# A graph layer over 50,000 nodes: the second weight applied before the edge sum, in a first pass over DRAM

## The reference

```python
_layernorm(x) = (x - mean) / sqrt(var + 1e-05)          # over the 256 features
# graph layer, on xn = _layernorm(x); edge_index = stack([src, dst])
agg  = segment_sum(xn[dst], src)                        # for each node, over its edges
mean = agg / maximum(segment_sum(1, src), 1)[:, None]
x = x + xn @ W1.T + b1 + mean @ W2.T + b2
# feed-forward, on h = _layernorm(x)
all_out = experts_mlp(h, ...)      # 4 experts, 256 -> 128 -> 64 -> 256, relu
shared  = shared_mlp(h, ...)       # 256 -> 256 -> 128 -> 256, relu
gates = softmax(h @ gW + gb); the two largest, softmax over them
x = x + shared + sum of the two chosen experts' outputs by those weights
```

## Time and profile before

| what | value |
|---|---|
| time, median of 3 runs | 4213.46 us (4186.71 to 4247.7) |
| span of the profiled execution | 4086.2 us |
| the profiled execution's own launch time | not given; the three runs lie 100.5 to 161.5 us above its span |
| instructions | 72214 |
| TensorE busy | 3755.7 us, 92% |
| VectorE busy | 3509.2 us, 86% |
| GpSimd busy | 2756.4 us, 67% |
| ScalarE busy | 2236.2 us, 55% |
| granted TensorE clock, mean | 0.955 |
| DMA, mean | 39 GB/s |

### The profile page before, as it was taken

The page is one execution under the profiler, slowest core; times in us unless marked ns, Lnnn a source line. Parts: engine busy times, 40 slices in busy tenths (PEclk is TensorE's granted clock), DMA queues, the critical chain, the costliest instruction groups (busy, mean ns, idle before and its releaser), DMA issues.

```text
span 4086.2 us, 72214 instructions
## 1 busy us (share of the span) xinstructions
PE 3755.7 (92%) x20644; PEld 2987.0 (73%) x20644; DVE 3509.2 (86%) x8557; ACT 2236.2 (55%) x4286; POOL 2756.4 (67%) x2275
## 2 busy tenths in 40 slices
PE   4677599999999999999999999999999999999998
PEld 2222387877788787777877788788878878778776
DVE  8999788888888888888888888888888888888886
ACT  1455355555565555555655555555655555555554
POOL 3044576777777777776777777777777777777762
PEclk6699899999999999999999999999999999999999
DMA  1000111111111111111111111111111111111110
GB/s 33 0 0 0 40 47 45 42 35 45 46 45 45 42 42 38 45 45 40 45 35 45 45 45 45 38 41 41 46 45 45 45 36 41 44 45 45 42 34 19
DMA packets 52637, 157.42 MB, mean 39 GB/s; under 512 B 13637, under 2 KB 14327, under 8 KB 52602
## 3 DMA queue, kind: packets, MB, share of 16 engines
q1 hardware_dynamic: 28602, 105.73, 7.7%
q0 software_dynamic: 24000, 51.29, 4.4%
HBM read 120.06 MB, written 51.20 MB: 42 GB/s over the span
## 4 chain that ended last, share of the span: by engine, by line
PE 44%; DVE 18%; issue 12%; POOL 8%; ACT 4%; another core or an unknown queue 2%; DVEq 1%; POOLq 0%; ACTq 0%
PE bank L1032 12%; PE bank L1008 10%; PE bank L985 9%; DVE h_lo L1256 5%; PE bank L866 5%; PE bank L925 4%; POOL l_var L774 3%; POOL l_rstd L784 3%; DVE x1n_sb L1314 3%; PE bank L959 2%; DVE x_sb L1191 2%; ACT h_hi L1096 1%; ACT xT_hi L915 1%; DVE l_mv L1303 1%
## 5 line engine op out<-in xcount | busy, mean ns | idle before, releaser
L826 POOL TENSOR_SCALAR e_oh<-iota_sb,cols 128x500 fp32r<-128x500 f32 x490 | 836.1, 1724 | 20.8 <-POOL cols L820 20.8
L985 PE MATMUL bank<-x1T_hi,wl_hl 128*128 128x500 f32 x2400 | 669.7, 394 | 0.0
L796 POOL DMA_INDIRECT rows<-in_x,slots x500 | 517.3, 1035 | 211.2 <-issue 98.8
L774 POOL TENSOR_SCALAR l_var<-l_mv 125x4 f32<-125x4 f32 x200 | 149.9, 749 | 693.4 <-DVE l_mv L1303 688.9
L1256 DVE TENSOR_TENSOR h_lo<-h1f,h_hi 128x500 fp32r<-128x500 f32 x600 | 525.6, 917 | 42.8 <-ACT h_hi L1096 32.3
L915 ACT CAST ag_hi<-bank 128x500 fp32r<-128x500 f32 x200 | 115.4, 577 | 815.8 <-PE bank L866 724.8
L1050 PE MATMUL bank<-wl_hl,h_hi 128*125 128x256 f32 x2400 | 534.3, 298 | 0.0
L985 PEld LDWEIGHTS bank<-x1T_hi,wl_hl 128*128 128x128 f32 x2400 | 442.5, 188 | 86.8
L1032 PE MATMUL bank<-h_hi,wl_hl 128*128 128x500 f32 x1200 | 410.0, 457 | 92.3 <-DVE h_lo L1256 92.3
L1089 ACT ACTIVATE h1f<-bank,bl_sb 128x500 f32<-128x500 f32 x600 | 407.8, 680 | 153.4 <-PE bank L985 84.3
L1314 DVE TENSOR_SCALAR x1n_sb<-x_sb,l_mv,l_rstd 125x256 f32<-125x256 f32 x400 | 343.7, 919 | 127.0 <-POOL l_rstd L784 127.0
(11 more groups left out here) (178 smaller groups left out, 9083.3 us busy)
## 6 DMA issues: line engine op xcount, KB each, us to landing
x_sb<-in_x SPq DMA_DIRECT2D x100, 500.0 KB
out<-out_sb SPq DMA_DIRECT2D x100, 500.0 KB
rows<-in_x,slots POOLq DMA_INDIRECT x500
st_wl<-in_wl SPq DMA_DIRECT2D x1, 768.0 KB
st_wl<-in_wl SPq DMA_DIRECT2D x2, 384.0 KB
st_w<-in_w1t SPq DMA_DIRECT2D x1, 256.0 KB
st_w<-in_w2t SPq DMA_DIRECT2D x1, 256.0 KB
st_b<-in_b SPq DMA_DIRECT2D x1, 256.0 KB
```

The source lines that it names most:

```text
L774: pool.tensor_scalar(L["var"][:], mv[:, :, 1], EPS, None, ALU.add).then_inc(S[f"{tag}_var_ready"], 1)
L796: pool.indirect_dma_start(out=rows[g.h][:, q, :], out_offset=None, in_=x, in_offset=bass.IndirectOffsetOnAxis(ap=slots[g.h][:, q:q + 1], a ...
L826: pool.tensor_scalar(e_oh[:, q, :], iota_sb[:], cols[:, q:q + 1], None, ALU.is_equal).then_inc(S["e_oh_ready"], 1)
L985: mm = pe.matmul(bank[L1_BANKS[t]][:, 0:GN], wl1_hl[:, w, f, t * P:(t + 1) * P], (x1T_hi, x1T_lo)[a][:, f, :], start=n == 0, stop=n == 5)
```

## The change

The program becomes two passes over the nodes.

First pass (from L211 of the changed kernel, all 100 groups written out without a loop). Per group g: SyncE loads x (`xs`, four buffers); VectorE takes the statistics (`stats`), GpSimd 1/sqrt, ScalarE normalises (`norm`); TensorE transposes and multiplies by W1 and W2 in node rows (`rows_of`, 48 matmuls of 256 columns and 4 for the bias); VectorE adds x and writes `ys` (y = x + xn W1 + b1 + b2), ScalarE copies `zs` (z = xn W2); SyncE stores both to DRAM (`y_d`, `z_d`). The sort is cut up and laid over these groups: five one-hot steps of totals in each of groups 0 to 15, two rank steps in each of groups 17 to 56. In place of the table by matmuls, each edge writes one 64-byte row (source, node column) into a table in DRAM (`tab_d`), at its slot, by 400 indirect DMAs of 125 rows, five in each of groups 20 to 99. The weights of the feed-forward block are split in groups 62 to 66.

Second pass, pipelined over groups i, i + 1, i + 2 and i + 3, a loop of U = 4 groups per pass: SyncE loads y and the group's part of the table; GpSimd gathers rows of z instead of x and makes the one-hots; the gathered rows need no layernorm; `sum_edges` is 40 matmuls of 256 or 258 columns that give node rows, the two extra columns of ones in `e_hi` giving the counts; x1 is made straight from the sum (`graph_vector`). `graph_layer`, the transposes of xn, the counts, and the separate bias add are gone. The gate logits are made in node rows (16 matmuls of 8 columns) and not transposed back. The bias and gate operands of layer 3 (`b3_r`, `selg_r`, `wT_r`) are padded with zeros to 128 rows.

The core of the diff:

```diff
-UNR = 4
+ROW = 16
+U = 4
+DX = D + 2
+G_TOT = 16
+G_RANK = G_TOT + 1
+G_SCAT = 20
+G_WTS = 62
+NSC = 8
+PER_G = E // EP // (NG - G_SCAT)
...
+                        for g in range(NG):
+                            sp.wait_ge(a_y, 2 * g + 2)
+                            sp.dma_start(y_v[g], ys[:, g % 2]).then_inc(s_y[g % 2], 16)
+                            if g + 4 < NG:
+                                load_x(g + 4)
+                            sp.wait_ge(a_z, 2 * g + 2)
+                            sp.dma_start(z_v[g], zs[:, g % 2]).then_inc(s_z[g % 2], 16)
...
+                            pool.indirect_dma_start(
+                                out=tab_d,
+                                out_offset=bass.IndirectOffsetOnAxis(ap=idx[:, n:n + 1], axis=0),
+                                in_=pair[:, 2 * n:2 * n + ROW], in_offset=None,
+                                bounds_check=NROW - 1, oob_is_err=False).then_inc(s_scat[n % NSC], 16)
...
+                        for g in range(NG):
+                            if g + 1 < NG:
+                                low(g + 1)
+                            if g + 2 < NG:
+                                neg_bias(g + 2)
...
+                            for n in steps[0:1]:
+                                if n + 2 < STEPS:
+                                    rank_onehot(n + 2)
+                                rank_select(n)
+                                if n:
+                                    rank_sum(n - 1)
+                            y_half(g, 0)
+                            if g + 3 < NG:
+                                stats(g + 3)
+                            for n in steps[1:2]:
+                                if n + 2 < STEPS:
+                                    rank_onehot(n + 2)
+                                rank_select(n)
+                                rank_sum(n - 1)
...
+                            y_half(g, 1)
...
-                                for f in range(FT):
-                                    mm = pe.matmul(o, hl[a][:, f, cols_], wt[:, w, f, :],
-                                                   start=n == 0, stop=n == 5)
-                                    n += 1
-                    mm.then_inc(S["gnn_done"], 1)
...
+                def sum_edges(k):
+                    s = S_ORDER[k]
+                    cols_ = slice(s * SP_, (s + 1) * SP_)
+                    for q in range(EQ):
+                        pe.matmul(bank[2 + s][0:SP_, 0:DX], e_oh[:, q, cols_], e_hi[:, q, :],
+                                  start=q == 0, stop=False)
+                        mm = pe.matmul(bank[2 + s][0:SP_, 0:D], e_oh[:, q, cols_], e_lo[:, q, :],
+                                       start=False, stop=q == EQ - 1)
+                    mm.then_inc(S["agg_done"], 1)
```

1985 lines of the change are left out of this document (980 added, 1005 removed).

## The result

The changed kernel takes 4292.4 us (median of 4 runs, 4289.4 to 4295.8) beside 4212.7 for the kernel before (4186.7 to 4247.7): ratio 1.019, 95% interval 1.014 to 1.024. It is slower, clear of no change, by 1.9% and not by the 6.3% of the forecast. The time lies inside the range; the size of the difference is a third of what was said.

What follows compares the result with a forecast made beforehand. TensorE bounds the groups now, VectorE the sort; DMA transfers and waits would bound the new first pass, TensorE the second. 1638 + 10 + 2703 = 4351 us, plus 127.3: 4478, 6.3% slower; own range 4300 to 4650, wider range 4150 to 4750.

Steps and rivals of the forecast that it cites:

- The median of the runs, 4213.5, lies 127.3 above the profiled span; I carry that over.: Last step, from span to time: 127.3 us added to the span of 4351, giving 4478.
- one group in two is long. So 34.3 is TensorE's work at full clock, and a pass of the loop costs 3.0 us more: Reading of the earlier profile's groups, 34.3 then 37.3 us: the extra 3.0 us priced as the loop's branch.
- 0.75 per group: Second pass: branch cost of 3.0 us spread over the four groups of a loop pass, bounds 0 and 1.5.
- The chain of 14.2: First pass: waits from y through x, statistics and half of y to the next y, 14.2 us per group.
- so the DMA sum decides by a little: 14.7: First pass, groups without rank steps: three transfers of 4.9 us on five DMA engines set the period, 14.7 us.
- Scatters: First pass: indirect writes of table rows add 0.7 us per group for 80 groups, 56 us.
- the seven terms of 25.6: Second pass, TensorE per group: transposes, layer 1 with gate weights, layer 2, edge sums, layer 3, logits, gate broadcast; 25.6 us.
- A: Rival: first pass streams well, 3.9 us per transfer, chain 12.2; time 4096, 2.8% faster; chance 0.24 with its milder form.
- B: Rival: DMA does not hold the first pass, transfers spread over 16 engines or overlap; time 3777; chance 0.05.
- C: Rival: stores and scatters bite in the first pass, 17.5 us per group and scatters 3 us; time 4886; chance 0.13.
- D: Rival: chain to the gate weights or a second stall per pass binds pass 2 at 28.5; time 4668; chance 0.09.
- E: Rival: a misplaced wait serialises the sort with the first pass, 437 us more; chance 0.02.

Runs made afterwards that it cites:

- before_again: The kernel before, unchanged, run and profiled again on chip 1: 3899.6 us (median of 10).
- stats_late: Changed kernel with stats(g + 3) moved behind the second half of y of group g: 3944.7 us on chip 1, ratio 1.011 to the kernel before.
- before_pad: Kernel before with only b3_r, selg_r and wT_r padded with zeros from 14 to 128 rows: 3975.4 us on chip 7 beside 3903.4.

## Why the prediction came out as it did

**The step that failed** is "The median of the runs, 4213.5, lies 127.3 above the profiled span; I carry that over." The runs lie 1.5 to 1.9 us above their spans, in both kernels. The 127 us are a difference between two executions of the kernel before, the profiled one and the timed ones; the traces show such differences as more or fewer long groups, but why this profile lies 100 us under the fastest of its timed runs is open. Of the 182 us between the forecast (4478) and the profiled launch (4295.8), 126 are this step. Without it the forecast is 4353, 3.3% slower than before.

**The step under it** is the reading of the earlier trace rows: "one group in two is long. So 34.3 is TensorE's work at full clock, and a pass of the loop costs 3.0 us more". The loop of two groups costs the kernel before nothing (34.04 throughout in before_again, 0.3 us per branch on all engines). The 1.60 us are a late semaphore update, some 11 us ahead of the long group; the 3.3 are a wait of 1.73, for a low part that GpSimd's addition held, and a stretch of half clock. One group in two was a fair count (53 of 99, most at one place of the pass), but the cost is not the branch's. The earlier trace rows itself could have told: its place is between two casts of one helper, which no branch parts. The price carried to the second pass, 0.75 per group, came out nearly right (3.4/4 = 0.85) for a reason that only the changed kernel has.

**First pass**: 1648 to the second pass by the sum, 1635 measured. Close, but by terms that were partly wrong and made up for each other:
- The chain of 14.2, with its 11.2 for x, is right to the tenth; with a rank step 16.2 was foretold and 16.0 measured.
- "so the DMA sum decides by a little: 14.7" is wrong. The sum is 11.8, and some 12.4 with the scatters (stats_late), since a transfer takes 3.9 and not 4.9. I took 4.9 from busy shares, and these don't measure throughput: the share is 0.31 at 108 GB/s here and 0.32 at 130 in stats_late, for the same packets of 4096 bytes, whose mean is 186 ns here and 161 there. Why they are slower where the load is waited for is not shown. The best microsecond of the earlier trace rows, 131 KB, was the true rate. 14.7 and 14.2 lay so near each other that only the experiments part them.
- Scatters: 0.7 foretold, 0.9 to 1.2 measured.
- TensorE's clock was 0.77 to 0.84, not "mostly 0.5"; it decides nothing there.

**Second pass**: 2703 foretold, 2659 measured. Period 26.0 for 26.6: of the seven terms of 25.6 none is off by more than 0.14 (the logits 1.66 for 1.8), and together they make 25.2; the wait of 0.3 ahead of the transposes was not there (25.2 for 25.9); the branch took 0.85 for 0.75. So the group without its graph layer was priced right as a whole; no run takes that layer out alone.

**Rivals**: A's transfer of 3.9 is what stats_late reaches, and A still did not come, because it let the chain fall with it to 12.2; the load had y ahead of it and took 11.3. B was right that spreading the transfers over 16 engines would matter (9.2 per group), and wrong that this kernel does so. C, D and E did not happen.

**Same or slower**: the change removes 9 us from every group (34.04 to 25.2) and puts 1635 us ahead of them in place of 437. How it compares depends on what the chip makes of the kernel before: 1.9% slower in the first runs and 1.7% on chip 3, where TensorE's updates come late, and 9.8% on chip 7, where they don't. That the time fell inside the range, and the direction was right, owes something to luck: the forecast took the kernel before to have one time, and on chip 7 the same changed kernel would have been slower by half as much again as foretold.

## What to carry to other kernels

Take the span and the launch time of one and the same execution before adding anything between them, and when runs of a kernel spread by over 1% look first for what in its own trace comes and goes. A kernel whose bound engine has no waits can be at an edge: here the last low part began 0.48 us before an instruction of GpSimd that would hold it for 2.1, and a small delay, or TensorE getting faster, brought waits and half clock. So look, beside each instruction of VectorE that TensorE waits for, at what GpSimd starts at that moment. And transfer 112 + 13 rows, not 125: this alone turned a change that loses 9.8% on chip 7 into one that wins 4.5% on chip 1, where the kernel before takes the same 3900, and with the wait for the load taken out of the store's chain and the loop written out it wins 9.6%.

## What the runs showed of the hardware that I had not expected

- On chips 3 and 12 and in the first trace semaphore updates of TensorE came up to some 2.4 us after the matmuls in a stretch of small ones, in the kernel before on chips 1 and 7 after 14 ns. The kernel before takes 5 to 8% more on the former (4112 and 4213 against 3900), the changed one nothing on chip 3.
- A VectorE instruction of 0.67 us (`h_lo`) that began beside GpSimd's `oh_pair<-e_oh` took 2.8 us, in 54 of 54 cases in the trace of before, 34 of 34 in before_pad and 2 of 2 in before_again; one of 0.40 (`x1n_sb`) beside `xb_sb<-x_sb,bias` took 2.5. Beside GpSimd's `e_oh<-iota_sb,cols` the same low parts take 0.67.
- A wait of TensorE of 1.6 to 1.9 us was followed by 3.4 us of half clock in 52 of 53 cases ahead of layer 2 in the trace of before, and in 42 of 130 in that of before_pad.
- On VectorE and ScalarE a branch cost 0.2 to 0.3 us with up to 255 of the engine's own instructions in the loop and 2.9 to 5.4 with 269 and more; on TensorE's queue 0.3 with 859.
- Five scatters of 125 rows of 64 bytes lengthened a group by 0.9 to 1.2 us where the load was waited for, and by 0.5 to 0.8 where it was not.
